# Routing work moved between the parts of the attention slots: variances, choice, slots and feature scaling

## The chip, the cores and the metric

The program runs on one core of one Trainium2 chip. The time is the device time of the whole program in microseconds (us). Of the kernel before three executions were timed.

## The reference, cut to what matters

The model has eight sublayers over `x` of shape 16 x 512 x 128. The change touches the third, attention with rotary positions, and the token routing of the fourth, a mixture of 8 experts, that the kernel computes inside the third.

```python
x = x + _L0_attn_a_ref(_layernorm(x), ...)
x = x + _L0_ffn_ref(_layernorm(x), ...)
x = x + _L0_attn_b_ref(_layernorm(x), Wq, Wk, Wv, Wo, bo)      # 16 heads of 64, causal
x = x + _L0_ffn_ref(_layernorm(x), centroids, ...)             # its routing is done in the line above
...
def _L0_ffn_ref(x, centroids, gamma, beta, W1, b1, W2, b2):
    feats = x.reshape(-1, x.shape[-1])
    scores = feats @ centroids.T
    expert = jnp.argmax(scores, axis=1)
    ...
    h = (xs - mu) * jax.lax.rsqrt(var + EPS) * g + b           # a second norm of feats
```

## The kernel before, in words

The stage is `rope_attention`. It goes over 16 batches (sequences of 512 tokens, 4 tiles of 128) times 4 groups of 4 heads, 64 groups in all. One group is one **slot** k, and a slot has eight **parts** j = 0 to 7. All five engines run the same loop `slots(body)`, unrolled in Python, each with a body of its own; the order in a body is the order of the instructions on that engine, and the engines meet only in semaphores. Nothing is scheduled by a compiler.

In a slot, PE (TensorE) projects queries, keys and values of group k (parts 0 to 5, L2924, L2920, and L2915 in parts 1 and 5 for the values), projects out group k - 3 (part 6, L2935), does one extra job in part 7, and beside that multiplies the scores of two head pairs (L2954), transposes probabilities (L2866) and multiplies them with the values (L2967). All of the projections and the extra jobs use one PSUM bank, `ps_r`. DVE (VectorE) multiplies with cosine and sine in parts 0, 2, 3 and 4 (L3086, L3087), masks the scores and takes their minima (L3078), copies transposed probabilities (L3092) and inverts sums (L3098). ACT (ScalarE) takes exponentials (L3012), copies the values in parts 1 and 5 (L3034), and copies probabilities and outputs (L3018, L3025). POOL (GpSimd) rotates (L2792, parts 2 and 4) and divides (L2799, four instructions of growing size per head pair).

The extra work comes every fourth slot. With k counted modulo 4 the slots are called here:

- **rank slot** (k = 2): DVE turns the scores of a batch into a choice (L3135, L3138, L3142, L3145), PE ranks it in part 7. In the same slots DVE measures the rows of the next batch for the first norm (`coming`, L3209, L3211, parts 0 to 3), takes the variance (L3214) and POOL its power (L2813) and the normed rows (L2818).
- **statistics slot** (k = 3): DVE measures the finished rows for the second norm (L3104, L3106, parts 0 to 3), takes two variances (L3110, L3111), and finishes the slot numbers of an earlier batch (L3154, L3157, L3161); POOL adds the bias (L2823, part 3) and raises to the power (L2829, `rooted`). PE turns the normed rows in part 7.
- **norm slot** (k = 0): POOL writes the features (L2837), PE turns them in part 7 (L2878), ACT copies them (L3050).
- **choose slot** (k = 1): PE multiplies with the centroids in part 7 (L2885), DVE copies the scores out of `ps_r` (L3124). ACT scales the features into the rows to send (L3063). POOL sends the rows of an older batch (L2850), DVE mixes in the expert output of the sublayer before (L520).

The core of the gate between ACT and PE:

```python
                    if front is not None and t == 1:
                        act.wait_ge(sg["v_in"], 2 * front + j // 4 + 1)
                        ...
                        nc.scalar.copy(v[...], ps_r[:]).then_inc(sg["v_ready"], 1)
                def project_out(q, front):
                    ...
                    wait(pe, sg["v_ready"], 2 * min(q + OUT + 1, QUADS))
```

Of the kernel before, what the change touches and what calls it, by code (L numbers as in the profile page):

```python
# [12 lines left out]
D = 128  # L13
NB, S = 16, 512
T = NB * S // P
EPS = 1e-5
# [2617 lines left out]
def rope_attention(core, name, made, kept, Wq, Wk, Wv, Wo, bo, cos_in, sin_in):  # L2634
# [20 lines left out]
    SCALE = CHOOSE  # L2655
    with ExitStack() as ctx:
# [77 lines left out]
        with nc.Block() as block:  # L2734
# [35 lines left out]
            def _(pool):  # L2770
# [31 lines left out]
                def body(j, t, s, front, score, value, out, batch, coming, mixing, routed):  # L2802
# [8 lines left out]
                    if coming is not None and j == 7:  # L2811
                        pool.wait_ge(sg["var_done"], coming + 1)
                        nc.gpsimd.tensor_tensor(rs[:], var[:], core.minus_half[:, 0:TC], ALU.pow).then_inc(sg["rs_done"], 1)  # L2813
# [10 lines left out]
                    if routed(STATS) is not None and j == 7:  # L2824
                        b = routed(STATS)
                        pool.wait_ge(sg["ve_done"], 2 * (b + 1))
                        wait(pool, sg["again_done"], b)
                        flat = lambda m: m[:].rearrange("p k c -> p (k c)")
                        nc.gpsimd.tensor_tensor(flat(rr), flat(ve), core.minus_half[:], ALU.pow).then_inc(sg["rooted"], 1)  # L2829
# [168 lines left out]
            def _(act):  # L2998
# [21 lines left out]
                def body(j, t, s, front, score, value, out, batch, coming, mixing, routed):  # L3020
# [34 lines left out]
                    if routed(SCALE) is not None and t == 2:  # L3055
                        b = routed(SCALE)
                        if j == 2:
                            act.wait_ge(sg["feats_done"], TC * (b + 1))
                            act.wait_ge(sg["again_done"], b + 1)
                            act.wait_ge(sg["consts"], NCONST)  # L3060
                            wait(act, sent[b % 2], 16 * TC * (b // 2))
                        for c in (0, 1) if j == 2 else (2, 3):
                            nc.scalar.activation(hx[:, b % 2, c, 0:D], feats[:, c, :], ACT.Copy, scale=again[:, c:c + 1]).then_inc(sg["h_done"], 1)  # L3063
# [3 lines left out]
            def _(dve):  # L3067
# [39 lines left out]

                def variances(b):
                    dve.wait_ge(sg["mean2_done"], TC * (b + 1))
                    nc.vector.tensor_scalar(ve[:, 0, :], mv2[:, :, 1], EPS, None, ALU.add).then_inc(sg["ve_done"], 1)  # L3110
                    nc.vector.tensor_scalar(ve[:, 1, :], mv2[:, :, 1], 1.0 + EPS, EPS * EPS, ALU.mult, ALU.add).then_inc(sg["ve_done"], 1)  # L3111
# [10 lines left out]
                def highest(b):  # L3122
                    dve.wait_ge(sg["scored"], b + 1)
                    nc.vector.tensor_copy(score_of[:].rearrange("p t e -> p (t e)"), ps_r[:, 0:TC * E]).then_inc(sg["score_kept"], 1)  # L3124
                    dve.wait_ge(sg["score_kept"], b + 1)
                    nc.vector.tensor_reduce(kept.top[:, b * TC:(b + 1) * TC], score_of[:], AX.X, ALU.max).then_inc(sg["top_done"], 1)

                def at_highest(b):
                    dve.wait_ge(sg["top_done"], b + 1)
                    nc.vector.tensor_tensor(ranked[:], score_of[:], by_expert(kept.top[:, b * TC:(b + 1) * TC]), ALU.is_equal).then_inc(sg["eq_done"], 1)  # L3130

                def choice(b, j):
                    if j == 2:
                        dve.wait_ge(sg["eq_done"], b + 1)
                        nc.vector.tensor_tensor(ranked[:], ranked[:], by_tile(kept.favour[:]), ALU.mult).then_inc(sg["rank_done"], 1)  # L3135
# [15 lines left out]
                def slots_of(b, j):  # L3151
# [6 lines left out]
                    if j == 7:  # L3158
# [4 lines left out]
                def body(j, t, s, front, score, value, out, batch, coming, mixing, routed):  # L3163
# [24 lines left out]
                    if routed(CHOOSE) is not None and j == 7:  # L3188
                        highest(routed(CHOOSE))
                    if routed(RANK) is not None:  # L3190
                        choice(routed(RANK), j)
                    if routed(STATS) is not None and j < TC:
                        stats(routed(STATS), j)
                    if routed(STATS) is not None and j == 7:
                        variances(routed(STATS))
                    if routed(SLOT) is not None:
                        slots_of(routed(SLOT), j)
# [5 lines left out]
                    if routed(CHOOSE) is not None and j == 7:  # L3203
                        at_highest(routed(CHOOSE))
# [59 lines left out]
```

## Time and profile before

| | |
|---|---|
| median of three executions | 3939.24 us |
| lowest, highest | 3928.66, 3944.43 us |
| the profiled execution | 3944.43 us, span 3942.7 us |
| PE busy over the span | 3455.3 us, 88% |
| DVE, ACT, POOL | 70%, 58%, 55% |
| the stage of the change | about 1190 to 2727 us of the span |

The span runs from the first to the last instruction that the profiler recorded. Busy time of PE is modelled from its instruction starts. In the rows below a line number Lnnn is a line of the kernel before. In a timeline the columns are the start and the duration in us, then engine, line, operation, output<-inputs, shapes and the count of merged instructions; in square brackets stands how long the engine sat idle before it and who released it. Small instructions of one engine overlap by some hundredths of a microsecond, so that the next can start before the one before is over. The granted clock (PEclk) is 1.00 at full speed, 2.4 GHz.

### The profile page before, as it was taken

To read this page: it belongs to the slowest core of one execution; us is meant where nothing else is said; L and a number is where in the kernel's file an instruction comes from. 1 tells how busy PE (TensorE), PEld (TensorE's weight loads), DVE (VectorE), ACT (ScalarE), POOL (GpSimd) and SP (SyncE) were. 2 spreads that over 40 slices of the span, in tenths; PEclk is the share of its full clock that TensorE was granted. 3 is DMA by queue.
4 is the path that set the end of the run, shared out by engine and by line. 5 is a ranking of instruction groups with operands and counts; after the bars stand their busy time and mean duration, and the time that the engine had idled before them with its cause. 6 is when DMAs were issued, how large, how long until landed. Compare 5 with 4: busy or idle time off the path is not lost. (4 is left out here: it accounts for less than half of the span.)

```text
span 3942.7 us, 89530 instructions
## 1 busy us (share of the span) xinstructions
PE 3455.3 (88%) x30494; PEld 2111.7 (54%) x30494; DVE 2757.4 (70%) x7236; ACT 2286.2 (58%) x5520; POOL 2169.0 (55%) x2263
## 2 busy tenths in 40 slices
PE   5999999985695999999999999995958885987678
PEld 1333333325592566566566566563946774775456
DVE  6888888856454778878888888873437884655565
ACT  2777777763243666666666666662436671864367
POOL 3333333315544777888887888874422332754275
PEclk7999999995697999999999999997979997987879
DMA  5434334413452222222222222222633332110001
GB/s 100 61 59 60 60 60 62 62 17 101 137 193 67 48 55 50 51 56 55 53 57 51 51 57 51 50 55 75 199 92 81 89 82 43 44 45 5 0 1 44
DMA packets 414451, 254.32 MB, mean 65 GB/s; under 512 B 251418, under 2 KB 340434, under 8 KB 412722
## 3 DMA queue, kind: packets, MB, share of 16 engines
q1 hardware_dynamic: 403316, 226.43, 25.0%
q0 software_dynamic: 10688, 22.17, 1.8%
q8 instruction: 251, 4.11, 0.4%
q14 instruction: 196, 1.61, 0.1%
HBM read 91.61 MB, written 45.94 MB: 35 GB/s over the span
## 5 line engine op out<-in xcount | busy, mean ns | idle before, releaser
L2799 POOL TENSOR_TENSOR ra_prob<-ra_prob,ra_inverse 128x256 f32<-128x256 f32 (+3 forms) x512 | 631.1, 1255 | 250.5 <-DVE ra_inverse L3098 249.3
L2577 DVE TENSOR_REDUCE ca_mx<-ca_ps_s 128x2 f32<-128x1024 f32 x512 | 600.6, 1211 | 120.4 <-PE ca_ps_s L2449 120.2
L3012 ACT ACTIVATE ra_prob<-ra_ps_s,ra_low 128x128 f32<-128x128 f32 (+3 forms) x1024 | 533.6, 532 | 228.5 <-DVE ra_low L3078 225.8
L2514 ACT ACTIVATE ca_pT<-ca_ps_p 128x512 f32<-128x512 f32 x1024 | 544.9, 600 | 204.6 <-PE ca_ps_p L2459 203.1
L3078 DVE CUSTOM_DVE_ANT_0 ra_ps_s<-ra_ps_s,ra_mask 128x128 f32<-128x128 f32 (+3 forms) x1024 | 479.9, 510 | 44.1 <-PE ra_ps_s L2954 43.8
L2449 PE MATMUL ca_ps_s<-ca_kst,ca_qst 128*128 128x512 bf16 x1024 | 393.0, 389 | 24.4 <-DMA ca_kst<-ca_bounce 10.9
L2459 PE MATMUL ca_ps_p<-ca_qst,ca_kst 128*128 128x512 bf16 x1024 | 386.7, 383 | 5.5 <-ACT ca_pT L2514 4.2
L3018 ACT COPY ra_probT<-ra_ps_t 128x512 f32<-128x512 f32 x384 | 227.2, 592 | 254.2 <-PE ra_ps_t L2866 254.2
L2866 PE MATMUL ra_ps_t<-ident,ra_prob 128*128 128x128 f32 x2560 | 350.1, 276 | 3.3 <-ACT ra_probT L3018 2.1
L2954 PE MATMUL ra_ps_s<-ra_kz,ra_qz 64*128 64x128 f32 (+3 forms) x2048 | 348.1, 458 | 3.8 <-DMA ra_kz<-ra_rot 2.9
L2792 POOL TENSOR_TENSOR ra_rot<-ra_prod 128x512 f32<-128x512 f32 x256 | 320.6, 1273 | 40.6 <-DVE ra_prod L3087 40.6
L2866 PEld LDWEIGHTS ra_ps_t<-ident,ra_prob 128*128 128x128 f32 x2560 | 291.0, 141 | 93.2 <-issue 60.1
L2967 PE MATMUL ra_ps_o<-ra_probT,ra_v 128*64 128x512 f32 (+3 forms) x2048 | 300.8, 436 | 0.0
L3086 DVE TENSOR_TENSOR ra_prod<-ra_ps_r,ra_cos 128x512 f32<-128x512 f32 x256 | 176.0, 687 | 174.3 <-PE ra_ps_r L2924 145.5
L2469 PE MATMUL ca_ps_o<-ca_pT,ca_vst 128*32 128x512 f32 x2048 | 272.8, 605 | 0.1
L2459 PEld LDWEIGHTS ca_ps_p<-ca_qst,ca_kst 128*128 128x128 bf16 x1024 | 98.2, 97 | 306.7 <-ACT ca_pT L2514 211.7
L2954 PEld LDWEIGHTS ra_ps_s<-ra_kz,ra_qz 64*128 64x128 f32 x2048 | 156.1, 187 | 157.5 <-issue 118.2
L2924 PE MATMUL ra_ps_r<-ra_xT,ra_w 128*128 128x512 f32 x384 | 220.4, 656 | 5.6 <-DVE ra_prod L3087 2.8
L2967 PEld LDWEIGHTS ra_ps_o<-ra_probT,ra_v 128*64 128x64 f32 x2048 | 132.4, 137 | 164.7 <-issue 164.0
L3012 ACT ACTIVATION_READ_ACCUMULATOR ra_prob<-ra_ps_s,ra_low 128x1 f32 x1024 | 211.4, 206 | 0.0
L3092 DVE COPY ra_probT<-ra_ps_t 128x512 f32<-128x512 f32 x256 | 176.7, 690 | 37.2 <-PE ra_ps_t L2866 35.1
L2449 PEld LDWEIGHTS ca_ps_s<-ca_kst,ca_qst 128*128 128x128 bf16 x1024 | 98.7, 98 | 142.7 <-DVE ca_mx L2577 64.6
(491 smaller groups left out, 7278.5 us busy)
## 6 DMA issues: line engine op xcount, KB each, us to landing
ra_qz<-ra_rot SPq DMA_DIRECT2D x512, 64.0 KB, 2.0
ra_kz<-ra_rot SPq DMA_DIRECT2D x512, 64.0 KB, 2.0
moe_w_own<-moe_w1T SPq DMA_DIRECT2D x71, 256.0 KB
moe_w_own<-router_w SPq DMA_DIRECT2D x71, 256.0 KB
ca_kst<-ca_bounce SPq DMA_DIRECT2D x256, 64.0 KB
ca_bounce<-ca_thirds SPq DMA_DIRECT2D x192, 64.0 KB
ca_qst<-ca_bounce SPq DMA_DIRECT2D x64, 192.0 KB
moe_hs<-moe_rows SPq DMA_DIRECT2D x71, 66.0 KB, 2.1
```

The source lines that it names most:

```text
L2449: ins = nc.tensor.matmul(out[:, k % 2 * 512:(k % 2 + 1) * 512], chunk(qst, P, h, a, qt), chunk(kst, P, h, a), start=True, stop=True)
L2459: nc.tensor.matmul(out[:], chunk(kst, P, h, a, kt), chunk(qst, P, h, a), start=True, stop=True).then_inc(sg["filled"], 1)
L2469: last = nc.tensor.matmul(ps_o[b * 32:(b + 1) * 32, :], vst[:, h % VRING, a, kt, :], pT[:, (NS * h + 4 * r + b) % PRING, :], start=(kt == ...
L2514: nc.scalar.activation(pT[:, (NS * hp + u) % PRING, :], ps_p[n % NP][:], ACT.Exp).then_inc(sg["drained"], 1)
L2577: nc.vector.tensor_reduce(mx[:, hm % 2, 2 * j:2 * j + 2], ps_s[m % 2][:].rearrange("p (b k) -> p b k", b=2), AX.X, ALU.max)\
L2792: nc.gpsimd.tensor_tensor(rot[:, front % 2, o, x, :], prod[:, o, 2 * x, :], prod[:, o, 2 * x + 1, :], op).then_inc(sg["rotated"], 1)
L2799: nc.gpsimd.tensor_tensor(at, at, inverse[:, n % PROB, 2 * tile:2 * tile + 2].unsqueeze(2).broadcast_to([P, 2, keys]), ALU.mult)\
L2866: last = nc.tensor.transpose(ps_t[f % 2][:, k * P:(k + 1) * P], prob[:, n % PROB, c, head, kt * P:(kt + 1) * P], core.ident[:])
L2954: last = nc.tensor.matmul(part(n, tile)[:, head, :], qz[half, n % RING, tile * P:keys], kz[half, n % RING, 0:keys], start=True, stop=True)
L2967: last = nc.tensor.matmul(ps_o[head * DH:(head + 1) * DH, kt * P:], v[:, n // 2 % VRING, kt, d:d + DH], probT[:, i, first:first + S - kt * P],
L3012: nc.scalar.activation(prob[:, n % PROB, tile, head, 0:keys], part(n, tile)[:, head, :], ACT.Exp, bias=low[:, n % PROB, at:at + 1], scale= ...
L3078: nc.vector.tensor_tensor_reduce(scored, scored, mask[:, S - (tile + 1) * P:], 1.0, BIGGEST, ALU.add, ALU.min, low[:, n % PROB, at:at + 1])\
```

## The change

No operation is added or dropped. On DVE the variance of the next batch and the two variances of the second norm move from part 7 to part 3. The reduction to the highest score and the comparison with it move from part 7 of the choose slot to parts 0 and 1 of the rank slot, the selection from part 5 to part 4, and the cast to slot numbers from part 7 to part 2. The slot number work now stands ahead of the statistics of the same part. On POOL the two powers move from part 7 to part 3 (first norm) and part 5 (second norm). On ACT the four scalings move from parts 2 and 6 of the choose slot (two each) to parts 4 to 7 of the norm slot (one each), each with a wait for its own tile of features.

```diff
-    SCALE = CHOOSE
...
-                    if coming is not None and j == 7:
+                    if coming is not None and j == 3:
                         pool.wait_ge(sg["var_done"], coming + 1)
                         nc.gpsimd.tensor_tensor(rs[:], var[:], core.minus_half[:, 0:TC], ALU.pow).then_inc(sg["rs_done"], 1)
...
-                    if routed(STATS) is not None and j == 7:
+                    if routed(STATS) is not None and j == 5:
                         b = routed(STATS)
                         pool.wait_ge(sg["ve_done"], 2 * (b + 1))
...
-                    if routed(SCALE) is not None and t == 2:
-                        b = routed(SCALE)
-                        if j == 2:
-                            act.wait_ge(sg["feats_done"], TC * (b + 1))
+                    if routed(NORM) is not None and j >= TC:
+                        b, c = routed(NORM), j - TC
+                        act.wait_ge(sg["feats_done"], TC * b + c + 1)
+                        if c == 0:
                             act.wait_ge(sg["again_done"], b + 1)
...
-                        for c in (0, 1) if j == 2 else (2, 3):
-                            nc.scalar.activation(hx[:, b % 2, c, 0:D], feats[:, c, :], ACT.Copy, scale=again[:, c:c + 1]).then_inc(sg["h_done"], 1)
+                        nc.scalar.activation(hx[:, b % 2, c, 0:D], feats[:, c, :], ACT.Copy, scale=again[:, c:c + 1]).then_inc(sg["h_done"], 1)
...
                     nc.vector.bn_aggr(mv2[:, c, :], parts2[:, c, :]).then_inc(sg["mean2_done"], 1)
-
-                def variances(b):
-                    dve.wait_ge(sg["mean2_done"], TC * (b + 1))
...
+                    if c == TC - 1:
+                        dve.wait_ge(sg["mean2_done"], TC * (b + 1))
+                        nc.vector.tensor_scalar(ve[:, 0, :], mv2[:, :, 1], EPS, None, ALU.add).then_inc(sg["ve_done"], 1)
+                        nc.vector.tensor_scalar(ve[:, 1, :], mv2[:, :, 1], 1.0 + EPS, EPS * EPS, ALU.mult, ALU.add).then_inc(sg["ve_done"], 1)
...
                 def choice(b, j):
+                    top = kept.top[:, b * TC:(b + 1) * TC]
+                    if j == 0:
+                        dve.wait_ge(sg["score_kept"], b + 1)
+                        nc.vector.tensor_reduce(top, score_of[:], AX.X, ALU.max).then_inc(sg["top_done"], 1)
+                    if j == 1:
+                        dve.wait_ge(sg["top_done"], b + 1)
+                        nc.vector.tensor_tensor(ranked[:], score_of[:], by_expert(top), ALU.is_equal).then_inc(sg["eq_done"], 1)
...
-                    if j == 5:
+                    if j == 4:
                         dve.wait_ge(sg["best_done"], b + 1)
                         wait(dve, sg["ranks_in"], b)
                         nc.vector.tensor_tensor(chosen[:], ranked[:], by_expert(best[:]), ALU.is_equal).then_inc(sg["chosen_done"], 1)
+                    if j == 5:
...
-                    if j == 7:
+                    if j == 2:
                         dve.wait_ge(sg["slot_f_done"], b + 1)
...
-                    if coming is not None and j == 7:
-                        dve.wait_ge(sg["mean_done"], TC * (coming + 1))
-                        nc.vector.tensor_scalar(var[:], mv[:, :, 1], EPS, None, ALU.add).then_inc(sg["var_done"], 1)
+                        if j == TC - 1:
+                            dve.wait_ge(sg["mean_done"], TC * (coming + 1))
+                            nc.vector.tensor_scalar(var[:], mv[:, :, 1], EPS, None, ALU.add).then_inc(sg["var_done"], 1)
```

On DVE in the rank slot, end of part 3 and start of part 4 (`ra_best` is the choice's maximum, `ra_prod` the products with cosine and sine), there stands before:

```order
L3138 TENSOR_REDUCE ra_best<-ra_ranked 128x4
L3209 BN_STATS ra_parts<-X 128x6
L3211 BN_AGGR ra_mv<-ra_parts 128x2
L3086 TENSOR_TENSOR ra_prod<-ra_ps_r,ra_cos 128x512
L3087 TENSOR_TENSOR ra_prod<-ra_ps_r,ra_sin 128x512
```

and in the changed kernel, at the same place:

```order
L3132 TENSOR_REDUCE ra_best<-ra_ranked 128x4
L3202 BN_STATS ra_parts<-X 128x6
L3204 BN_AGGR ra_mv<-ra_parts 128x2
L3207 TENSOR_SCALAR ra_var<-ra_mv 128x4
L3084 TENSOR_TENSOR ra_prod<-ra_ps_r,ra_cos 128x512
L3085 TENSOR_TENSOR ra_prod<-ra_ps_r,ra_sin 128x512
```

The variance has moved ahead of the multiplications of part 4. On DVE in the statistics slot, end of part 2 and of part 3, there stands before (`ra_inverse` are the inverted sums, `ra_parts` and `ra_mv` the statistics):

```order
L3098 RECIPROCAL ra_inverse<-ra_total 128x4
L3104 BN_STATS ra_parts<-X 128x6
L3106 BN_AGGR ra_mv<-ra_parts 128x2
...
L3104 BN_STATS ra_parts<-X 128x6
L3106 BN_AGGR ra_mv<-ra_parts 128x2
L3086 TENSOR_TENSOR ra_prod<-ra_ps_r,ra_cos 128x512
```

and now:

```order
L3096 RECIPROCAL ra_inverse<-ra_total 128x4
L3156 CAST ra_slot<-ra_slot_f 128x4
L3102 BN_STATS ra_parts<-X 128x6
L3104 BN_AGGR ra_mv<-ra_parts 128x2
...
L3102 BN_STATS ra_parts<-X 128x6
L3104 BN_AGGR ra_mv<-ra_parts 128x2
L3107 TENSOR_SCALAR ra_ve<-ra_mv 128x4
L3108 TENSOR_SCALAR ra_ve<-ra_mv 128x4
L3084 TENSOR_TENSOR ra_prod<-ra_ps_r,ra_cos 128x512
```

So both variances moved ahead of the multiplications of part 4, and the cast into part 2. On ACT in the norm slot, parts 4 and 5 (`ra_prob` the exponentials, `ra_v` the copied values), before:

```order
L3018 COPY ra_probT<-ra_ps_t 128x512
L3012 ACTIVATE ra_prob,ra_total<-ra_ps_s,ra_low 128x128
L3012 ACTIVATE ra_prob,ra_total<-ra_ps_s,ra_low 128x256
L3034 COPY ra_v<-ra_ps_r 128x512
L3018 COPY ra_probT<-ra_ps_t 128x512
```

and now:

```order
L3017 COPY ra_probT<-ra_ps_t 128x512
L3011 ACTIVATE ra_prob,ra_total<-ra_ps_s,ra_low 128x128
L3011 ACTIVATE ra_prob,ra_total<-ra_ps_s,ra_low 128x256
L3061 ACTIVATE ra_hx<-ra_feats,ra_again 128x128
L3033 COPY ra_v<-ra_ps_r 128x512
L3017 COPY ra_probT<-ra_ps_t 128x512
```

One scaling has moved ahead of the copy of the values in part 5; the three others stand at the ends of parts 5, 6 and 7.

## Rows read from the trace of the kernel before

**Rows 1.** Engines by stretch of the stage (columns named in the first line).
```profile
core 0: us, PE busy (x) PEld busy (x) DVE busy (x) ACT busy (x) POOL busy (x), PEclk, DMA share, GB/s
1900.00:2000.00 100.00, 99.51 (x645) 61.21 (x643) 80.61 (x259) 63.85 (x192) 81.91 (x71) 1.00 0.23 56
```

**Rows 2.** Waits of PE, 1390 to 2560 us.
```profile
PE ra_ps_r L2935 <- ACT ra_v L3034: 2.8, 13, 0.3
```

**Rows 3.** Timeline of PE: start, duration, line, out<-in, wait before.
```profile
1359.10 2.02 PE L2935 MATMUL ra_ps_r<-ra_wo,ra_oT 128*128 128x128 f32 x16
...
1381.05 2.02 PE L2935 MATMUL ra_ps_r<-ra_wo,ra_oT 128*128 128x128 f32 x16
...
1881.24 2.02 PE L2935 MATMUL ra_ps_r<-ra_wo,ra_oT 128*128 128x128 f32 x16
...
1904.51 2.02 PE L2935 MATMUL ra_ps_r<-ra_wo,ra_oT 128*128 128x128 f32 x16 [0.20 <-ACT ra_v L3034]
...
1926.92 2.02 PE L2935 MATMUL ra_ps_r<-ra_wo,ra_oT 128*128 128x128 f32 x16
...
1947.68 1.03 PE L2915 MATMUL ra_ps_r<-ra_wv,ra_xT 128*128 128x256 f32 x4
...
1949.61 2.02 PE L2935 MATMUL ra_ps_r<-ra_wo,ra_oT 128*128 128x128 f32 x16
```

**Rows 4.** Timeline of ACT: the second value copy in three slots.
```profile
1903.67 0.58 ACT L3034 COPY ra_v<-ra_ps_r 128x512 f32<-128x512 f32 x1
...
1926.09 0.58 ACT L3034 COPY ra_v<-ra_ps_r 128x512 f32<-128x512 f32 x1
...
1948.78 0.58 ACT L3034 COPY ra_v<-ra_ps_r 128x512 f32<-128x512 f32 x1
```

**Rows 5.** Timeline of DVE, the rank slot.
```profile
1896.76 0.87 DVE L3135 TENSOR_TENSOR ra_ranked<-ra_ranked,router_favour 128x32 f32<-128x32 f32 x1
...
1900.82 0.18 DVE L3211 BATCH_NORM_AGGREGATE ra_mv<-ra_parts 128x2 f32<-128x6 f32 x1
1900.92 0.67 DVE L3086 TENSOR_TENSOR ra_prod<-ra_ps_r,ra_cos 128x512 f32<-128x512 f32 x1
```

**Rows 6.** Timeline of DVE, the statistics slot.
```profile
1922.89 0.18 DVE L3106 BATCH_NORM_AGGREGATE ra_mv<-ra_parts 128x2 f32<-128x6 f32 x1
1923.31 0.69 DVE L3086 TENSOR_TENSOR ra_prod<-ra_ps_r,ra_cos 128x512 f32<-128x512 f32 x1 [0.24 <-PE ra_ps_r L2924]
```

**Rows 7.** Timeline of DVE: operations of part 7 that move to part 3.
```profile
1910.29 0.46 DVE L3214 TENSOR_SCALAR ra_var<-ra_mv 128x4 f32<-128x4 f32 x1
...
1932.60 0.56 DVE L3110 TENSOR_SCALAR ra_ve<-ra_mv 128x4 f32<-128x4 f32 x1
1933.07 0.16 DVE L3111 TENSOR_SCALAR ra_ve<-ra_mv 128x4 f32<-128x4 f32 x1
```

**Rows 8.** Timeline of POOL over both slots.
```profile
1894.26 3.32 POOL L2799 TENSOR_TENSOR ra_prob<-ra_prob,ra_inverse 128x768 f32<-128x768 f32 x2 [4.71 <-DVE ra_inverse L3098]
...
1900.00 1.62 POOL L2799 TENSOR_TENSOR ra_prob<-ra_prob,ra_inverse 128x256 f32<-128x256 f32 x2
...
1922.61 1.60 POOL L2799 TENSOR_TENSOR ra_prob<-ra_prob,ra_inverse 128x256 f32<-128x256 f32 x2
1924.17 1.27 POOL L2823 TENSOR_TENSOR X<-X,ra_bias 128x512 f32<-128x512 f32 x1
...
1931.52 1.61 POOL L2799 TENSOR_TENSOR ra_prob<-ra_prob,ra_inverse 128x256 f32<-128x256 f32 x2 [0.34 <-DVE ra_inverse L3098]
```

**Rows 9.** Timeline of ACT: two scalings where they stand now.
```profile
1975.28 0.69 ACT L3063 ACTIVATE ra_hx<-ra_feats,ra_again 128x128 f32<-128x128 f32 x2
```

**Rows 10.** Timeline, the end of the stage.
```profile
2703.50 1.67 POOL L2829 TENSOR_TENSOR ra_rr<-ra_ve,minus_half 128x8 f32<-128x8 f32 x1 [11.74 <-DVE ra_ve L3111]
```

**Rows 11.** Groups by line and shape, 1390 to 2560 us (line engine op shapes xcount | busy, mean ns).
```profile
L2799 POOL TENSOR_TENSOR ra_prob<-ra_prob,ra_inverse 128x512 f32<-128x512 f32 x102 | 106.2, 1041 | 0.0
L2799 POOL TENSOR_TENSOR ra_prob<-ra_prob,ra_inverse 128x256 f32<-128x256 f32 x102 | 62.8, 616 | 12.7 <-DVE ra_inverse L3098 12.0
```

More of the change, by code:

```diff
@@ L3106, in stats @@
                     nc.vector.bn_aggr(mv2[:, c, :], parts2[:, c, :]).then_inc(sg["mean2_done"], 1)
-                def variances(b):
-                    dve.wait_ge(sg["mean2_done"], TC * (b + 1))
-                    nc.vector.tensor_scalar(ve[:, 0, :], mv2[:, :, 1], EPS, None, ALU.add).then_inc(sg["ve_done"], 1)
-                    nc.vector.tensor_scalar(ve[:, 1, :], mv2[:, :, 1], 1.0 + EPS, EPS * EPS, ALU.mult, ALU.add).then_inc(sg["ve_done"], 1)
+                    if c == TC - 1:
+                        dve.wait_ge(sg["mean2_done"], TC * (b + 1))
+                        nc.vector.tensor_scalar(ve[:, 0, :], mv2[:, :, 1], EPS, None, ALU.add).then_inc(sg["ve_done"], 1)
+                        nc.vector.tensor_scalar(ve[:, 1, :], mv2[:, :, 1], 1.0 + EPS, EPS * EPS, ALU.mult, ALU.add).then_inc(sg["ve_done"], 1)
                 def second_norm(b):
@@ L3120, in second_norm @@
                     nc.vector.tensor_copy(hx[:, b % 2, :, D].bitcast(mybir.dt.int32), kept.ids[:, b * TC:(b + 1) * TC]).then_inc(sg["ids_done"], 1)
[L3122 to L3130, printed above, removed]
-                def choice(b, j):
+                def choice(b, j):
+                    top = kept.top[:, b * TC:(b + 1) * TC]
[5 more added lines that the diff above has]
+                        nc.vector.tensor_tensor(ranked[:], score_of[:], by_expert(top), ALU.is_equal).then_inc(sg["eq_done"], 1)
                     if j == 2:
@@ L3188, in body @@
                     if routed(CHOOSE) is not None and j == 7:
-                        highest(routed(CHOOSE))
+                        b = routed(CHOOSE)
+                        dve.wait_ge(sg["scored"], b + 1)
+                        nc.vector.tensor_copy(score_of[:].rearrange("p t e -> p (t e)"), ps_r[:, 0:TC * E]).then_inc(sg["score_kept"], 1)
                     if routed(RANK) is not None:
                         choice(routed(RANK), j)
+                    if routed(SLOT) is not None:
+                        slots_of(routed(SLOT), j)
                     if routed(STATS) is not None and j < TC:
                         stats(routed(STATS), j)
[L3194 to L3197, printed above, removed]
                     if routed(NORM) is not None and j == 0:
@@ L3202, in body @@
                         made.mix(X, mixing * TC + t, fresh[:, t, :]).then_inc(sg["mixed"], 1)
-                    if routed(CHOOSE) is not None and j == 7:
-                        at_highest(routed(CHOOSE))
                     if coming is not None and j < TC:
```

## The prediction

> **What bounds the kernel now.** I first read the busy table of the stage that the change touches (rope attention, about 1190 to 2727 us of the span), stretch by stretch. The reader should see in it that TensorE has no room: in 1900 to 2000 us PE is busy 99.51 of 100 us at a granted clock of 1.00, while DVE is at 81, ACT at 64 and POOL at 82 [rows 1]. So work saved on DVE, ACT or POOL is worth nothing here, and work put on them costs nothing unless PE is made to wait for it.
>
> Second, the waits of PE. Between 1390 and 2560 us one is left: the output projection (L2935) waits 13 times, 2.8 us in all, for ACT's copy of the values (L3034) [rows 2]. That names the chain on which PE has no slack: in each slot PE multiplies the values (L2915, part 5), ACT copies them, PE projects out (part 6). The copy starts at 1903.67, 1926.09 and 1948.78 [rows 4], and L2935 at 1904.51, 1926.92 and 1949.61 [rows 3]: 0.83 to 0.84 us later each time. So the projection is released by that copy in every slot, also where the view shows no wait. In front of the copy on ACT stand the exponentials of part 4, released by DVE's minima, which stand on DVE behind the multiplications L3086 and L3087 of part 4. **Whatever delays DVE at the end of part 3, or ACT in part 4, delays PE by the same amount, and PE never gets it back.**
>
> Third, I looked at slot lengths, as distances between starts of L2935 [rows 3]. Before any routing 1359.10 to 1381.05 is 21.95 us; 1881.24 to 1904.51 (with the choosing) is 23.27, 1904.51 to 1926.92 (with the ranking) is 22.41, 1926.92 to 1949.61 (with the turned rows) 22.69. The pattern repeats every four slots.
>
> Fourth, small DVE operations last longer when POOL is at work. L3135 takes 0.87 us, from 1896.76 to 1897.63, and POOL's pair of divisions runs from 1894.26 to 1897.58. L3110 takes 0.56, to 1933.16, and POOL's pair ends at 1933.13; L3111 right behind it takes 0.16 [rows 5, 7, 8]. L3214 takes 0.46. So these wait until POOL's running instruction is over. The Trainium skill, SBUF — State Buffer, "Who interferes with whom", says that a DVE instruction with two inputs in SBUF, or a tensor_scalar in a two-port mode, is blocked by a GpSimd instruction for the whole of that instruction. The trace agrees, with 0.56 against 0.16 us.
>
> **The change part by part**, by slots k modulo 4. In the rank slot (k = 2 mod 4) the next batch is also measured for its norm; in the statistics slot (3) the second norm is measured; then come the norm slot (0) and the choose slot (1).
>
> *Rank slot, DVE.* The variance (L3214) moves from part 7, where DVE then waits for PE anyway, to the end of part 3, straight ahead of L3086. The last aggregate before it is written at 1901.00 (1900.82 + 0.18), and L3086 now starts at 1900.92 without idle time before it [rows 5]: no slack. POOL's pair from 1900.00 consists of a division of 0.62 and one of 1.04 us [rows 8, 11], so the second runs until 1901.62. The variance asks at about 1901.05, gets through at 1901.60, and L3086 starts at about 1901.6: 0.68 us late. The bounds are 0.2 (it never waits: about the 0.16 of L3111 [rows 7], rounded up) and 0.87 (the wait of L3135). I take 0.68, since the POOL pair does not move. The reduction (part 0) and the comparison (part 1) added ahead of it fall before L3135, which waits for POOL's end anyhow and swallows them. The selection L3142 moves from part 5 to part 4, behind the minima; its delay, up to one rotation of POOL, meets the copy of part 5, which PE needs only in part 7. Cost 0.
>
> *Statistics slot, DVE.* Two operations (L3110, L3111) come to the end of part 3. Here L3086 is at 1923.31 after 0.24 us of idle time; the last aggregate is written at 1923.07 [rows 6]. POOL's pair from 1922.61 changes instruction at about 1923.2 and ends at 1924.21 [rows 8, 11]. The slot cast, now in part 2 ahead of the statistics, adds between 0.1 and 0.87 us there (again L3135) less what slack there is. With or without it the request comes just about or after 1923.2, and the two get through at 1924.2; L3086 then starts at about 1924.26: 0.95 us late. Bounds: 0.15 (they slip in at 1923.2: 0.35 of work less 0.24 idle, rounded up) and 0.95 + 1.27 = 2.2 (POOL's bias addition, queued at 1924.17 [rows 8], gets between them). I take 0.95.
>
> *Norm slot, ACT.* The four scalings leave the choose slot, where two in a row cost 0.69 us [rows 9] in ACT's idle time ahead of part 3 and part 7, and one each stands in parts 4 to 7 of the norm slot. The one in part 4 is directly ahead of the value copy. That copy starts at 1948.78, and PE's values end at 1948.71 (1947.68 + 1.03) [rows 3, 4]: slack 0.07. A scaling adds 0.35 (0.69 / 2), so the copy and PE are 0.28 us late. Bounds 0 and 0.35. Its input (first features, POOL part 1) is long there. The other three meet idle time: 0.
>
> *POOL.* The two powers move from part 7 to parts 3 and 5. Their results are wanted a slot later. In part 3 the power stands ahead of the second rotation, which waits for L3087 anyway. In part 5 it stands ahead of the divisions of part 7. Ahead of each slot's first big division POOL idles (4.71 us at 1894.26) [rows 8], which takes it up. Cost 0; if POOL ran without this idle time it would be one power per move, 1.67 [rows 10].
>
> *Removed from part 7 on DVE:* the variance operations and the comparison. DVE waits for PE's first projection of the next slot there. Gain 0.
>
> *Head and tail.* At the end of the stage the chain is serial: statistics, the power (POOL had idled 11.74 us before it) [rows 10], features. Two small slot operations of about 0.16 each (as L3111 [rows 7]) now stand among the last statistics. With their waits I estimate 0.5 us once, between 0.3 and 1.
>
> **Sum.** The rank slot has 13 full cases (batches 3 to 15), plus two early ones without L3135 at about 0.2: 13 x 0.68 + 0.4 = 9.2. The statistics slot has 15 (k = 7 to 63): 15 x 0.95 = 14.3. The norm slot has 14 (k = 8 to 60): 14 x 0.28 = 3.9. With the tail, 9.2 + 14.3 + 3.9 + 0.5 = 28 us. The profiled execution took 3944.43 us (span 3942.7, 1.7 around it), so that run becomes 3972. It was the slowest of three; the median is 3939.24, 5.2 less. For the median I forecast **3967 us**.
>
> **The rivals.**
> - *The small operations hardly wait.* For: bounds above; only one shape of these was seen at a changed time. Against: 0.56 and 0.46 in part 7. Rank 0.2, statistics 0.15, norm 0.28: 15 x 0.2 + 15 x 0.15 + 3.9 = 9 us, 3948.
> - *POOL gets between the two variance operations.* For: the bias addition is queued there. Against: L3111 followed L3110 at once, but POOL had nothing ready then [rows 7]. 15 x 1.27 = 19 more: 47 us, 3986. The Trainium skill, SBUF — State Buffer, "Who interferes with whom", has the lock held per instruction, so by it POOL may take it between the two; no run here shows who wins.
> - *Not slower: the spread loosens the gate.* The mechanism is DVE's order in the rank slot: if the added comparison shifts L3135 into the gap before POOL's big division at 1894.26, L3135 no longer waits, DVE reaches L3086 of part 4 up to 0.7 us (0.87 less 0.16) early, the variance is paid out of that, and the wait of 0.20 us at L2935 goes too [rows 2, 3, 5]. With the variances of the statistics slot in gaps as well, all of PE's 2.8 us of waits come back: 3936. It decides only if both happen in every batch, so it is unlikely.
> - *Nothing moves.* If the copy of the values has hidden slack, the delays vanish: 3939. Against: the constant 0.83 to 0.84.
>
> **How the numbers follow.** Forecast 0.50 (its own range 3958 to 3976), hardly waiting 0.25, POOL between 0.12, loosened 0.08, nothing 0.05. The range from 3944 to 3990 takes in the first three. Half a per cent, 20 us, is about what a measurement of this kernel can tell from no change; slower by more than that is most of the forecast's 0.50 and all of the 0.12, and 0.60 stands. Loosened is under the limit, so faster gets 0.03; the same 0.37.
>
> **What would show it.** Slots ending in L2935 grow: the 23.27 that ends in the rank slot by 0.7, the 22.41 by about 1, the 22.69 by 0.3; PE's waits for ACT's value copy become about 40 instead of 13. The variances at part 3 last 0.5 us or more, and L3086 of part 4 has none of its 0.24 idle left. I am wrong if slots keep their lengths, if L2935 no longer starts 0.84 after the copy, or if the variance takes 0.16.

## The result, and the profile after

The changed kernel takes 3980.61 us (median of six, 3976.04 to 3986.67), the kernel before 3941.97 us in the same runs (3928.66 to 3944.93). The ratio is 1.0104, with a 95% interval of 1.0087 to 1.0121: slower by about 39 us. The forecast for the median was 3967, the range 3944 to 3990.

The profiled execution has a span of 3980.8 us. PE is busy to 97 of 100 us where it was busy to 99.51 [rows 1], still at a granted clock of 1.00 (same columns):

```profile
1900.00:2000.00 100.00, 97.23 (x615) 58.26 (x614) 81.67 (x247) 61.17 (x184) 80.18 (x70) 1.00 0.23 55
```

The waits of PE in 1390 to 2600 us of the changed kernel, the whole view. Before there was one row, of 2.8 us [rows 2]:

```profile
PE ra_ps_r L2914 <- DVE ra_prod L3085: 22.9, 25, 1.6
PE ra_ps_r L2934 <- ACT ra_v L3033: 10.4, 37, 0.3
PE ra_ps_r L2934 <- issue: 0.2, 1, 0.2
```

L2934 is the output projection (L2935 before) and waits for the value copy (L3033) 37 times instead of 13. The larger row is new: PE's matmul of the values in part 5 (L2914) waits for DVE's multiplications of part 4 (L3085) directly, up to 1.6 us. The two share the PSUM bank, and the kernel has this matmul wait for the semaphore `multiplied`.

The output projections of one cycle of slots, norm, choose, rank, statistics and norm, in the timeline of PE:

```profile
1875.37 2.02 PE L2934 MATMUL ra_ps_r<-ra_wo,ra_oT 128*128 128x128 f32 x16 [0.32 <-ACT ra_v L3033]
...
1898.06 2.02 PE L2934 MATMUL ra_ps_r<-ra_wo,ra_oT 128*128 128x128 f32 x16
...
1919.71 1.13 PE L2914 MATMUL ra_ps_r<-ra_wv,ra_xT 128*128 128x256 f32 x4 [0.32 <-DVE ra_prod L3085]
...
1921.97 2.02 PE L2934 MATMUL ra_ps_r<-ra_wo,ra_oT 128*128 128x128 f32 x16 [0.26 <-ACT ra_v L3033]
...
1944.18 1.13 PE L2914 MATMUL ra_ps_r<-ra_wv,ra_xT 128*128 128x256 f32 x4 [1.55 <-DVE ra_prod L3085]
...
1946.47 2.02 PE L2934 MATMUL ra_ps_r<-ra_wo,ra_oT 128*128 128x128 f32 x16 [0.29 <-ACT ra_v L3033]
...
1969.45 2.02 PE L2934 MATMUL ra_ps_r<-ra_wo,ra_oT 128*128 128x128 f32 x16 [0.32 <-ACT ra_v L3033]
```

Read the distances between starts of L2934 against those of before [rows 3]. Into the rank slot 1898.06 to 1921.97 is 23.91 us (before 23.27), into the statistics slot 24.50 (22.41), into the norm slot 22.98 (22.69), into the choose slot 22.69 (22.69). Two of the four slots hold nearly all of the loss.

DVE at the end of part 3 and the start of part 4, first the rank slot, then the statistics slot. The rows of before are [rows 5, 6]:

```profile
1917.64 0.18 DVE L3204 BATCH_NORM_AGGREGATE ra_mv<-ra_parts 128x2 f32<-128x6 f32 x1
1917.86 0.60 DVE L3207 TENSOR_SCALAR ra_var<-ra_mv 128x4 f32<-128x4 f32 x1
1918.38 0.68 DVE L3084 TENSOR_TENSOR ra_prod<-ra_ps_r,ra_cos 128x512 f32<-128x512 f32 x1
...
1936.91 0.76 DVE L3156 CAST ra_slot<-ra_slot_f 128x4 uint32<-128x4 f32 x1
...
1940.76 0.18 DVE L3104 BATCH_NORM_AGGREGATE ra_mv<-ra_parts 128x2 f32<-128x6 f32 x1
1940.97 0.73 DVE L3107 TENSOR_SCALAR ra_ve<-ra_mv 128x4 f32<-128x4 f32 x1
1941.62 1.31 DVE L3108 TENSOR_SCALAR ra_ve<-ra_mv 128x4 f32<-128x4 f32 x1
1942.85 0.68 DVE L3084 TENSOR_TENSOR ra_prod<-ra_ps_r,ra_cos 128x512 f32<-128x512 f32 x1
```

and POOL beside it:

```profile
1916.83 1.60 POOL L2798 TENSOR_TENSOR ra_prob<-ra_prob,ra_inverse 128x256 f32<-128x256 f32 x2
...
1934.32 3.32 POOL L2798 TENSOR_TENSOR ra_prob<-ra_prob,ra_inverse 128x768 f32<-128x768 f32 x2 [3.02 <-DVE ra_inverse L3096]
...
1940.07 1.61 POOL L2798 TENSOR_TENSOR ra_prob<-ra_prob,ra_inverse 128x256 f32<-128x256 f32 x2
1941.64 1.27 POOL L2822 TENSOR_TENSOR X<-X,ra_bias 128x512 f32<-128x512 f32 x1
```

The variance of the rank slot (L3207) lasts 0.60 us, to 1918.46; POOL's divisions end at 1918.43. The cast (L3156) lasts 0.76, to 1937.67; POOL's pair ends at 1937.64. The first variance of the statistics slot (L3107) lasts to 1941.70, where the divisions end at 1941.68. The second (L3108) asks then, but POOL has gone on with the bias addition (L2822), 1941.64 to 1942.91, and L3108 is over at 1942.93. Only then can DVE multiply.

On ACT in the same slot the exponentials of part 4 wait for DVE's minima, and the copy of the values stands behind them:

```profile
1944.80 0.37 ACT L3011 ACTIVATE ra_prob<-ra_ps_s,ra_low 128x128 f32<-128x128 f32 x1 [1.99 <-DVE ra_low L3076]
...
1945.61 0.58 ACT L3033 COPY ra_v<-ra_ps_r 128x512 f32<-128x512 f32 x1
```

The delay of DVE thus reaches PE twice: at the values, which end at 1945.31 (1944.18 + 1.13), and at the projection, which starts 0.86 us after the copy.

By groups over the whole stage (count, then min/median/max in ns):

```profile
L3107 DVE TENSOR_SCALAR ra_ve<-ra_mv x16: 169/732/743, 1378.1 to 2745.3; 128x4 f32<-128x4 f32 x16
L3108 DVE TENSOR_SCALAR ra_ve<-ra_mv x16: 157/1315/1317, 1378.2 to 2745.4; 128x4 f32<-128x4 f32 x16
L3207 DVE TENSOR_SCALAR ra_var<-ra_mv x16: 169/604/615, 1207.8 to 2576.8; 128x4 f32<-128x4 f32 x16
L3136 DVE TENSOR_TENSOR ra_chosen<-ra_ranked,ra_best x16: 191/924/931, 1451.4 to 2755.4; 128x32 bf16<-128x32 f32 x16
```

Medians of 732, 1315 and 604 ns for operations whose shortest cases take 157 to 191: it happens in nearly every cycle. The first cycle (slot 7) has no cast yet, and tells the parts apart:

```profile
1378.09 0.17 DVE L3107 TENSOR_SCALAR ra_ve<-ra_mv 128x4 f32<-128x4 f32 x1
1378.17 1.05 DVE L3108 TENSOR_SCALAR ra_ve<-ra_mv 128x4 f32<-128x4 f32 x1
```
```profile
1377.58 1.62 POOL L2798 TENSOR_TENSOR ra_prob<-ra_prob,ra_inverse 128x256 f32<-128x256 f32 x2
1379.15 1.28 POOL L2822 TENSOR_TENSOR X<-X,ra_bias 128x512 f32<-128x512 f32 x1
```

L3107 asks 0.51 us after the pair begins, slips in where the small division (0.62 us [rows 11]) gives way to the large one, and takes 0.17. L3108 then waits for the large one, 1.05 us, and ends at 1379.22, just after the bias addition has begun (1379.15) but not held by it. In the statistics slot shown above L3107 asks 0.90 us after its pair begins (1940.97 less 1940.07), 0.4 us later. The first variance misses the point between the divisions, and the second meets the bias addition. The cast of part 2 is the likely reason for the 0.4 us: it waits 0.6 us there, and DVE then has no idle time up to L3107. No run moved the cast alone, so its share is argued from this one cycle.

Slot 63 has the cast but no bias addition, since no batch is left, and its second variance is short:

```profile
2693.56 0.73 DVE L3107 TENSOR_SCALAR ra_ve<-ra_mv 128x4 f32<-128x4 f32 x1
2694.20 0.16 DVE L3108 TENSOR_SCALAR ra_ve<-ra_mv 128x4 f32<-128x4 f32 x1
```

ACT in the norm slot: where [rows 4] had the copy at 1948.78 straight behind the exponentials, there stands now

```profile
1968.24 0.20 ACT L3011 ACTIVATION_READ_ACCUMULATOR ra_prob<-ra_ps_s,ra_low 128x1 f32 x1
1968.33 0.40 ACT L3061 ACTIVATE ra_hx<-ra_feats,ra_again 128x128 f32<-128x128 f32 x1
1968.62 0.58 ACT L3033 COPY ra_v<-ra_ps_r 128x512 f32<-128x512 f32 x1
```

and the projection starts 0.83 us after the copy (1969.45 less 1968.62), as before.

### The profile page after: what moved, and what is told of

It is laid out like the page before. It is cut to its first block and busy times, and to the rows that moved or that the text cites. A ratio compares the mean times of both kernels' runs of the same rounds, so it can differ in the third digit from the quotient of the medians.

```text
span 3980.8 us, 89435 instructions
## 1 busy us (share of the span) xinstructions
PE 3441.1 (86%) x30399; PEld 2107.8 (53%) x30494; DVE 2792.3 (70%) x7236; ACT 2289.0 (58%) x5520; POOL 2169.1 (54%) x2263
## 5 line engine op out<-in xcount | busy, mean ns | idle before, releaser
L2449 PE MATMUL ca_ps_s<-ca_kst,ca_qst 128*128 128x512 bf16 x991 | 380.4, 390 | 35.5 <-DVE ca_mx L2577 14.4
L2459 PE MATMUL ca_ps_p<-ca_qst,ca_kst 128*128 128x512 bf16 x962 | 362.8, 382 | 7.1 <-ACT ca_pT L2514 4.8
```

The lines of the kernel that those rows point to most:

```text
L2449: ins = nc.tensor.matmul(out[:, k % 2 * 512:(k % 2 + 1) * 512], chunk(qst, P, h, a, qt), chunk(kst, P, h, a), start=True, stop=True)
L2459: nc.tensor.matmul(out[:], chunk(kst, P, h, a, kt), chunk(qst, P, h, a), start=True, stop=True).then_inc(sg["filled"], 1)
```

## The experiments

All were timed in five rounds beside the kernel before on the same chip. Since the chips differ by a few us, ratios are to be compared; the changed kernel is at 1.0104. The table has the intervals between output projections that end in the named slot, in one cycle in the middle of the stage.

| kernel | rank | statistics | norm | choose | ratio to before (95%) |
|---|---|---|---|---|---|
| before | 23.27 | 22.41 | 22.69 | 22.69 | 1 |
| changed | 23.91 | 24.50 | 22.98 | 22.69 | 1.0104 (1.0087 to 1.0121) |
| x1 second-norm variances back | 23.92 | 22.47 | 22.97 | 22.69 | 1.0033 (1.0023 to 1.0042) |
| x2 first-norm variance back | 23.27 | 24.47 | 22.98 | 22.69 | 1.0091 (1.0076 to 1.0107) |
| x3 scalings back | 23.91 | 24.48 | 22.68 | 22.69 | 1.0088 (1.0072 to 1.0103) |
| x4 bias in part 6 | 23.92 | 23.32 | 22.98 | 22.69 | 1.0068 (1.0054 to 1.0081) |
| x5 before, choice moved only | 23.27 | 22.49 | 22.69 | 22.70 | 1.0007 (0.9998 to 1.0016) |
| x6 reciprocal for the variances | 23.91 | 22.74 | 22.98 | 22.69 | 1.0046 (1.0033 to 1.0059) |
| x7 before, favours in part 0 | 23.09 | 22.42 | 22.69 | 22.70 | 0.9996 (0.9985 to 1.0006) |
| x8 before, scalings moved only | 23.27 | 22.41 | 22.98 | 22.69 | 1.0012 (1.0002 to 1.0021) |
| x9 before, scores ahead of projection | 23.22 | 22.55 | 22.82 | 22.83 | 1.0024 (1.0014 to 1.0034) |
| x10 changed, the same | 23.81 | 24.37 | 22.82 | 22.83 | 1.0112 (1.0092 to 1.0133) |
| x11 x7 and x9 | 23.22 | 22.55 | 22.82 | 22.83 | 1.0024 (1.0009 to 1.0038) |
| x12 changed, powers back only | 23.91 | 24.47 | 22.98 | 22.69 | 1.0105 (1.0087 to 1.0124) |

(For x3 and x12 the rank interval is that of the neighbouring cycles; in the one shown it was 24.00 and 24.01.)

### x1 to x3: one part of the change undone at a time

x1:
```diff
-                    if c == TC - 1:
-                        (wait for mean2_done, the two tensor_scalar on ve)
+                    if routed(STATS) is not None and j == 7:
+                        variances(routed(STATS))
...
-                    if routed(STATS) is not None and j == 5:
+                    if routed(STATS) is not None and j == 7:
```


> The changed kernel with only the two variances of the second norm (and POOL's power on them) back in part 7 of the statistics slot. Port theory (a small DVE operation waits until POOL's running instruction is over, and DVE then starts the multiplications of part 4 late): the interval into the statistics slot falls from 24.4 to about 22.4 us, so 13 x 2.02 + 2 x 0.85 = 28 us less than the changed kernel, about 3953. Rival (the added instructions cost their own 0.16 us and a semaphore each, the rest comes from POOL's powers or the other moves): 15 x 0.3 = 5 us less, about 3976.

x2:
```diff
-                    if coming is not None and j == 3:
+                    if coming is not None and j == 7:
                         pool.wait_ge(sg["var_done"], coming + 1)
...
-                        if j == TC - 1:
+                    if coming is not None and j == 7:
                             dve.wait_ge(sg["mean_done"], TC * (coming + 1))
```


> The changed kernel with only the variance of the first norm (and POOL's power on it) back in part 7 of the rank slot. Port theory: the interval into the rank slot falls from 23.9 to 23.27, 13 x 0.64 = 8.3 us less, about 3972; it adds to the other parts. Rival (the choice's operations, now spread over parts 0 to 4, delay the rank slot): nothing, 3981.

x3:
```diff
-                    if routed(NORM) is not None and j >= TC:
-                        b, c = routed(NORM), j - TC
+                    if routed(SCALE) is not None and t == 2:
+                        b = routed(SCALE)
```


> The changed kernel with only ACT's scalings back in the choose slot. Gate theory (the scaling in part 4 stands ahead of the value copy): the interval into the norm slot falls from 22.98 to 22.69, 14 x 0.29 = 4 us less, about 3976.5. Rival (norm slot late because of something carried over from the statistics slot): the interval stays 22.98.

Measured medians: 3953.69, 3977.22 and 3975.37 us, beside 3940.25 for the kernel before. From the changed kernel's 1.0104 that is 0.71% (28 us), 0.13% (5 us) and 0.16% (6 us) less; the last two differ from the expected 8 and 4 by less than the intervals of the ratios (each about 0.15% or 6 us either way). In the traces each undoes its own interval and no other: 24.50 to 22.47, 23.91 to 23.27, 22.98 to 22.68. So the costs add, and about 28 of the 39 us belong to the two variances of the statistics slot.

### x4: POOL's bias addition out of the way

```diff
-                    if batch is not None and j == 3:
+                    if batch is not None and j == 6:
                         pool.wait_ge(sg["x_normed"], TC * (batch + 1))
```


> The changed kernel with POOL's bias addition moved from part 3 to part 6 of the statistics slot, nothing on DVE touched. Port theory with the port given up between the two variances: the second variance no longer finds POOL at work and falls from 1.31 to about 0.16 us, the interval into the statistics slot from 24.4 to about 23.2, 13 x 1.2 = 16 us less, about 3965. Rival (DVE's own instructions or the powers cost it): no change, 3981.

3967.22 us, ratio 1.0068: 0.36% or 14 us less, by moving an instruction of another engine. DVE in the statistics slot of this kernel:

```profile
1933.86 0.73 DVE L3107 TENSOR_SCALAR ra_ve<-ra_mv 128x4 f32<-128x4 f32 x1
1934.51 0.15 DVE L3108 TENSOR_SCALAR ra_ve<-ra_mv 128x4 f32<-128x4 f32 x1
1934.58 0.68 DVE L3084 TENSOR_TENSOR ra_prod<-ra_ps_r,ra_cos 128x512 f32<-128x512 f32 x1
```

L3107 still waits for the divisions, 0.73 us, but L3108 takes 0.15 instead of 1.31. The interval falls by 1.18. This shows that the second variance was held by the bias addition: what stands next in POOL's queue got in between two DVE operations.

### x6: the same places, another operation

```diff
-                        nc.vector.tensor_scalar(ve[:, 0, :], mv2[:, :, 1], EPS, None, ALU.add).then_inc(sg["ve_done"], 1)
-                        nc.vector.tensor_scalar(ve[:, 1, :], mv2[:, :, 1], 1.0 + EPS, EPS * EPS, ALU.mult, ALU.add).then_inc(sg["ve_done"], 1)
+                        nc.vector.reciprocal(ve[:, 0, :], mv2[:, :, 1]).then_inc(sg["ve_done"], 1)
+                        nc.vector.reciprocal(ve[:, 1, :], mv2[:, :, 1]).then_inc(sg["ve_done"], 1)
```


> The changed kernel with both variances of the second norm computed by DVE's reciprocal instead of its tensor_scalar, in the same place, same shape, same semaphores; this changes the scale of the features and of what is sent, so the output is another. The inverted sums use reciprocal beside POOL's work all the time at 0.17 us. Port theory: both take 0.16 to 0.17 us, L3084 of part 4 starts about 1.7 us earlier, the interval into the statistics slot falls from 24.4 to about 22.7, 13 x 1.7 = 22 us less, about 3958. Rival (position and order alone cost it): unchanged, 3981.

3954.11 us, ratio 1.0046: 0.58% or 23 us less. The groups of this kernel:

```profile
L3107 DVE RECIPROCAL ra_ve<-ra_mv x16: 178/178/179, 1373.6 to 2717.2; 128x4 f32<-128x4 f32 x16
L3108 DVE RECIPROCAL ra_ve<-ra_mv x16: 145/146/147, 1373.7 to 2717.3; 128x4 f32<-128x4 f32 x16
```

Their longest is 179 ns, with POOL's divisions under way as before:

```profile
1927.21 0.18 DVE L3107 RECIPROCAL ra_ve<-ra_mv 128x4 f32<-128x4 f32 x1
1927.31 0.15 DVE L3108 RECIPROCAL ra_ve<-ra_mv 128x4 f32<-128x4 f32 x1
1927.37 0.66 DVE L3084 TENSOR_TENSOR ra_prod<-ra_ps_r,ra_cos 128x512 f32<-128x512 f32 x1
```
```profile
1926.29 1.63 POOL L2798 TENSOR_TENSOR ra_prob<-ra_prob,ra_inverse 128x256 f32<-128x256 f32 x2
```

Same place, same shape, same semaphores, POOL at work from 1926.29 to 1927.92, and no wait. So it is the kind of operation that meets POOL, not the place in the order as such. Of the 0.33 left in the interval (22.74 against 22.41), 0.06 is there in x1 too, without the two; the other 0.27 is what two more instructions cost there when nothing holds them. In slot 7, where no cast has used up DVE's slack, they cost 0.01.

### x12: POOL's powers alone

```diff
-                    if coming is not None and j == 3:
+                    if coming is not None and j == 7:
...
-                    if routed(STATS) is not None and j == 5:
+                    if routed(STATS) is not None and j == 7:
```


> The changed kernel with only POOL's two powers back in part 7; DVE's variances stay in part 3. Port theory: the powers have no share in the cost, the intervals stay 23.9, 24.4 and 22.98, 3981. Rival (POOL's powers ahead of the second rotation or of the divisions delay PE): the intervals into the rank and the statistics slots fall, up to 1.0 and 1.7 us each.

Ratio 1.0105 (3991.10 us beside 3947.91, on a chip where both were slower): no difference that the time could tell, and the intervals are those of the changed kernel (23.91, 24.47, 22.98). The powers have no share.

### x5 and x8: one part of the change alone on the kernel before

x5, the choice and the slot numbers alone:
```diff
                 def choice(b, j):
+                    if j == 0: (reduction to the highest, was part 7 of the choose slot)
+                    if j == 1: (comparison with it, the same)
...
-                    if j == 5:
+                    if j == 4:
                         (selection)
...
-                    if j == 7:
+                    if j == 2:
                         (cast to slot numbers, ahead of the statistics)
```
x8, the scalings alone:
```diff
-                    if routed(SCALE) is not None and t == 2:
-                        b = routed(SCALE)
+                    if routed(NORM) is not None and j >= TC:
+                        b, c = routed(NORM), j - TC
+                        act.wait_ge(sg["feats_done"], TC * b + c + 1)
```

> The kernel before with only the choice and the slot numbers moved (parts 0, 1, 2 and 4), all variances, powers and scalings as before. Sum theory: these cost nothing, though the cast and the selection last 0.7 to 0.9 us longer: 3942, within 2 us. Rival (they eat the slack of part 3): the statistics slot gets longer by 0.3, 5 us more.

> The kernel before with only ACT's four scalings moved to the norm slot. Gate theory: the interval into the norm slot 22.69 to 22.98, 14 x 0.29 = 4 us more, 3946. Rival (it costs only beside the other moves): no change.

x5: 3938.92 us, ratio 1.0007: no difference beyond the noise, though the selection waits 0.93 us and the cast 0.76 in it too; the intervals are those of before within 0.08. These waits met slack and cost almost nothing. The cast is not free everywhere, though: by the comparison with slot 7 it pushes the variances of the changed kernel onto the bias addition. x8: 3941.94 us, ratio 1.0012 (1.0002 to 1.0021), 5 us, and its interval into the norm slot is 22.98. The cost of the scalings does not need the other moves.

### x7: the opposite move

```diff
                 def choice(b, j):
-                    if j == 2:
+                    if j == 0:
                         dve.wait_ge(sg["eq_done"], b + 1)
...
-                    if j == 3:
+                    if j == 1:
                         dve.wait_ge(sg["rank_done"], b + 1)
```


> The kernel before with the product with the favours moved from part 2 to part 0 of the rank slot, where POOL has nothing to do for 4.7 us, and the maximum from part 3 to part 1. Port theory: the product takes 0.16 instead of 0.87 us, DVE is on time in part 3, PE's wait of 0.20 us goes: up to 13 x 0.26 = 3 us less, 3938. Rival (DVE waits for PE somewhere in between anyway): no change.

3937.29 us beside 3936.06, ratio 0.9996 (0.9985 to 1.0006): too small to be told by the time. In its trace the product takes

```profile
L3135 DVE TENSOR_TENSOR ra_ranked<-ra_ranked,router_favour x16: 185/188/192, 1440.8 to 2713.4; 128x32 f32<-128x32 f32 x16
```

instead of 0.87 us, no wait of PE is left in 1390 to 2600 us, and the interval into the rank slot is 23.09, 0.18 less. It is the one version whose trace beats both kernels, by 13 x 0.18 = 2 us. No run here could confirm that as a time, and the 3 us that I had expected are not shown.

### x9, x10, x11: slack for the gate

```diff
+                    if score is not None and j == 6:
+                        scores(2, score)
                     if out is not None and j == 6:
                         project_out(out, front)
...
-                        for tile in (2, 3):
+                        for tile in (2, 3) if j == 2 else (3,):
                             scores(tile, score)
```


> The kernel before with one change on PE: in part 6 the scores of tile 2 (about 0.6 us of matmuls) stand ahead of the output projection instead of behind it, so that the projection comes 0.6 us after ACT's value copy could release it. Gate theory: the projection no longer waits for the copy in any slot; PE's 0.20 us in the rank slots and the 0.19 us it loses in every slot because the projection's weights cannot load early go: 63 x 0.19 + 2.8 = 15 us less, 3923. Rival (the 0.19 us belong to switching between the two kinds of matmul, not to the wait): only the 2.8 us, or a loss of some us where the job of part 7 now waits for DVE's addition.

> The changed kernel with the same change on PE. If the value copy were the only gate, all three costs would go: 3925. I expect two gates: the norm slot's 0.29 and the difference 0.64 less 0.32 of the rank slot go, while the wait of PE's values for DVE's multiplications (0.32 in the rank, 1.56 in the statistics slot) stays: 13 x (0.32 + 1.56) = 24 us above x9, about 3948. Rival (the delays come back through the wait for the addition): above 3960.

> The kernel before with both changes that took waits from PE: the scores of tile 2 ahead of the output projection, and the product with the favours in part 0. Gate theory: as x9, since the projection has slack anyway, 3923; rival (each is worth its own): 3 us less than x9.

x9: 3948.79 us, ratio 1.0024: slower, and my expectation of 15 us less was wrong. No wait of PE is left in 1390 to 2600 us, but a slot without routing is 22.24 us instead of 21.95. The trace of x9 around the projection:

```profile
1929.57 0.92 PE L2954 MATMUL ra_ps_s<-ra_kz,ra_qz 64*128 64x384 f32 x4
1930.41 2.05 PE L2935 MATMUL ra_ps_r<-ra_wo,ra_oT 128*128 128x128 f32 x16
1932.30 0.60 PE L2866 MATMUL ra_ps_t<-ident,ra_prob 128*128 128x128 f32 x4
1932.83 1.13 PE L2954 MATMUL ra_ps_s<-ra_kz,ra_qz 64*128 64x512 f32 x4
1933.89 0.66 PE L2944 MATMUL ra_ps_r<-ident,ra_xn 128*128 128x128 f32 x4
```

The two halves of the scores take 0.84 and 1.06 us from start to start, 1.90 in all, where the whole group in part 2 takes 1.70, as the next two rows of the same kernel show:

```profile
1942.85 1.77 PE L2954 MATMUL ra_ps_s<-ra_kz,ra_qz 64*128 64x384 f32 x8
1944.55 1.08 PE L2920 MATMUL ra_ps_r<-ra_xT,ra_w 128*64 128x512 f32 x4
```

So 0.20 of the 0.29 us lies in the split group itself. That one more change between kinds of matmul costs it is the likely reading, not a tested one.

What I had taken for a hidden wait of 0.19 in every slot is smaller, and not in every slot. In the kernel before, the projection starts 0.68 or 0.69 us after the copy in slots 4 to 8 and 0.83 or more from slot 9 on. In slot 6 the copy stands here and the projection at 1359.10 [rows 3]:

```profile
1358.42 0.58 ACT L3034 COPY ra_v<-ra_ps_r 128x512 f32<-128x512 f32 x1
```

x9 makes slots 4 to 8 longer by 0.28 or 0.29 us, but those from 9 to 63, the rank slots aside, only by 0.10 to 0.15. So about 0.15 us a slot did come back with the slack; the split costs more than that. From slot 9 on the kernel has the projection wait for signals of the routing as well (`routing_read`); whether these make the 0.15 was not tested.

x10 answers the question of the gate all the same: 3980.52 us, ratio 1.0112. Against x9 its norm slot is level (22.82 and 22.82), so the scaling costs nothing once the projection has slack, while the rank slot is 0.59 and the statistics slot 1.82 longer. That is 31 us over 13 cycles, where I had expected 24 from the waits alone. Its waits:

```profile
PE ra_ps_r L2914 <- DVE ra_prod L3087: 24.5, 26, 1.6
```

There are two gates behind DVE's multiplications, then: the value matmul waits for them directly, and behind it the copy for the projection. x11 is 1.0024 like x9: with slack at the projection the earlier product is worth nothing more.

## Why the prediction was right, point by point

- *PE has no slack, and part 4 is the gate.* Right for the slack: every delay of L3086 showed up in PE, and x1, x2, x3 and x8 change only the interval that the step named. The path was named in part only. I had DVE's delay reach PE by way of the minima, the exponentials and ACT's copy. The values of part 5 also wait for the multiplications directly: 22.9 of the 33.5 us of waits in the changed kernel are there. x10 takes the copy's part away, and 0.59 of the 0.64 and 1.82 of the 2.09 us remain. The distance of 0.83 to 0.84 between copy and projection is no constant either; it is 0.68 in slots 4 to 8.
- *Rank slot, 0.68 a case, 13 cases.* Measured 0.64 (23.27 to 23.91). Of the two early cases, for which I had 0.2 each, slot 6 cost nothing (21.95 to 21.96); slot 2 lies in the start of the stage and can't be told apart. So the step is 13 x 0.64 = 8.3 us for a forecast of 9.2.
- *Norm slot, 0.28 a case, 14 cases.* Measured 0.29, so 4.1 us for 3.9, confirmed by x3 and x8.
- *Statistics slot, 0.95 a case.* This is the term that was mis-sized. Thirteen cases cost 2.02 to 2.09 (22.41 to 24.50 in the cycle shown). The two others cost 0.83 (slot 7, no cast) and 0.88 (slot 63, no bias addition): 13 x 2.06 + 1.7 = 28.5 us for 14.3. With one of the two, cast or bias, the 0.95 was about right; x4 says the same (0.91 of cost left with the bias gone). I had written that the cast did not matter here, and had given the forecast to the way in which the bias did not either; together they cost 2.06. What I had taken as the likeliest way, both variances through at the end of the divisions, is how the first goes; the second is held for the 1.27 us of the bias addition. That was the second rival, with 0.12 of the chance and 3986 us. x4 takes this away alone and gets back 1.18 a case. Before the run no row showed who goes first when both wait; POOL's rows did show that it went from the divisions to the bias addition without idle time [rows 8], and the rival deserved more than 0.12. The Trainium skill, SBUF — State Buffer, "Who interferes with whom", says the shared port is held for a whole instruction by whichever engine issues first. The trace agrees as to the length of the waits (0.73 and 1.31 against 0.16 us).
- *The choice, the cast and the powers at no cost.* Right for the choice and the cast without the variances (x5 is at 1.0007) and for the powers (x12 at 1.0105 beside 1.0104). By slot 7 wrong for the cast beside the variances. The selection's wait (0.93) was foreseen at up to one rotation.
- *Tail.* The last projection starts at 2739.56 instead of 2697.63, 41.9 us later, and the last row is sent at 2761.71 instead of 2719.57, 42.1: 0.2 for the 0.5 estimated. Another 0.3 stands in the interval that ends in slot 65 (16.51 to 16.80); x8 has it and x3 has not, so it is a scaling, which no term had counted.

Sum by the measured terms: 8.3 + 28.5 + 4.1 + 0.3 + 0.2 = 41.4 us; 0.7 us were there before the first of these slots. The spans differ by 38.1 us, since other stages of this execution ran some us shorter, and the medians by 38.6. That DVE's small operations are held by POOL and that PE pays was right, and the range of 3944 to 3990 held. The forecast's own range of 3958 to 3976 did not: the 28 us were 11 short of the 38.6, by the one term, and the 3980.61 us are nearer to the rival's 3986 than to 3967. That the whole range held is owed to the rival, which it took in.

## What to carry to other kernels

Where an engine is busy without a gap, look for the instructions of the others that it waits for by a few hundredths of a microsecond, and keep everything small out of the stretch ahead of them: ahead of such a gate an operation of 0.16 us cost up to 1.2 us (x4), while the choice and the cast alone, moved where DVE had slack, cost less than 0.1 a slot (x5). Price a small DVE operation by what POOL runs at that moment, and two in a row by what POOL has queued next, too. To spread work evenly over the parts of a pipeline was no gain here; part 7, where everything stood, was the part where DVE had time.

## What the runs showed of the hardware

- DVE's tensor_scalar, tensor_tensor with both inputs in SBUF, and cast of 4 to 32 elements a partition waited for the end of POOL's running tensor_tensor (in the rows shown they took 0.60 to 1.31 us, against 0.15 to 0.19 where they did not wait). Reciprocal in the same place did not (at most 0.18 in x6), nor did the statistics just before it (0.26 to 0.29 in all 64 cases of L3102). Between two tensor_scalar of DVE, POOL's next queued instruction went first in all 13 cycles that had the bias addition queued there.
- A wait of PE costs more than the view of waits shows. In x10 the wait shown in the rank slot is 0.32 us and the interval is 0.59 longer than in x9; in the statistics slot 1.56 and 1.82. The weight loads begin only at the release too. PEld in the changed kernel, whose idle time there (1.79) is 0.24 longer than that of PE (1.55):

```profile
1944.17 0.73 PEld L2914 LDWEIGHTS ra_ps_r<-ra_wv,ra_xT 128*128 128x128 f32 x4 [1.79 <-DVE ra_prod L3085]
```

That this load is the whole of the difference was not tested by itself.

- Splitting one group of matmuls by another kind cost 0.29 us a slot on PE where no wait was there before (x9: 22.24 against 21.95, slots 4 to 8).
